# Flamingo block on one core: Wv and Wout loaded in halves, row statistics on GpSimd, a step's scales in one chain

## The reference

```python
x = x + tanh(g_xattn) * ((context @ Wv) @ Wout + bout)     # attention with that mask
h = layernorm(layernorm(x)) * ln1_g + ln1_b                # 256 wide
h = gelu(fake_quant(h) @ fake_quant_weight(w1).T + b1)     # 1024 wide
h = layernorm(h) * ln2_g + ln2_b
x = x + tanh(g_ffn) * (fake_quant(h) @ fake_quant_weight(w2).T + b2)
```

## Time and profile before

| | us |
|---|---|
| median of three runs | 402.39 |
| the profiled execution, its own time | 400.17 |
| its span, first to last instruction | 398.4 |
| VectorE busy | 330.2 (83%) |
| TensorE busy | 304.1 (76%) |
| ScalarE busy | 277.9 (70%) |
| GpSimd busy | 220.9 (55%) |
| mean granted TensorE clock | 0.949 of 2.4 GHz |

### The profile page before, as it was taken

The page is one execution under the profiler, slowest core; times in us unless marked ns, Lnnn a source line. Parts: engine busy times, 40 slices in busy tenths (PEclk is TensorE's granted clock), DMA queues, the critical chain, the costliest instruction groups (busy, mean ns, idle before and its releaser), DMA issues. The chain is left out here.

```text
span 398.4 us, 5821 instructions
## 1 busy us (share of the span) xinstructions
PE 304.1 (76%) x1690; PEld 187.9 (47%) x1690; DVE 330.2 (83%) x794; ACT 277.9 (70%) x446; POOL 220.9 (55%) x118
## 2 busy tenths in 40 slices
PE   2887295868888888888888888888888766758364
PEld 2776153434646464646464646464646342414043
DVE  0389366888999999999999999999999995957782
ACT  1314447678697979797979797979797968678431
POOL 4021444829484848484848484848485858454600
PEclk9999689989999999999999999999999996969669
DMA  7665404119183828383838383838270707062635
GB/s 226 244 225 181 132 0 130 56 53 185 54 186 107 190 102 182 108 183 110 184 107 184 108 183 109 180 111 172 67 170 18 170 17 160 26 115 71 135 77 160
DMA packets 97686, 51.56 MB, mean 129 GB/s; under 512 B 86535, under 2 KB 88768, under 8 KB 97654
## 3 DMA queue, kind: packets, MB, share of 16 engines
q1 hardware_dynamic: 96758, 51.14, 50.7%
q10 hardware_dynamic: 896, 0.04, 0.1%
HBM read 21.78 MB, written 8.41 MB: 76 GB/s over the span
## 5 line engine op out<-in xcount | busy, mean ns | idle before, releaser
L337 POOL TENSOR_TENSOR y<-u,g_bc 128x1024 f32<-128x1024 f32 x64 | 150.3, 2368 | 62.5 <-DVE parts L594 49.7
L694 DVE TENSOR_TENSOR y<-y,slot_c 128x1024 f32<-128x1024 f32 x64 | 77.7, 1214 | 9.9 <-PE slot_c L965 9.8
L698 DVE TENSOR_REDUCE amax<-y 128x1 f32<-128x1024 f32 x64 | 78.1, 1220 | 2.2
L432 ACT ACTIVATE q<-y,s 128x1024 f16<-128x1024 f32 x64 | 69.8, 1139 | 11.5 <-DVE s L725 11.5
L459 ACT ACTIVATE junk<-u,usum 128x1024 bf16<-128x1024 f32 x64 | 73.5, 1149 | 2.1
L1003 PE MATMUL bank_f<-w2T,q2T 128*128 128x256 f16 x512 | 66.1, 276 | 2.6 <-DVE res L745 2.4
L320 POOL TENSOR_TENSOR rstd<-var,half_neg 128x8 f32<-128x8 f32 x18 | 29.5, 1641 | 69.0 <-DVE var L645 56.6
L965 PE MATMUL slot_c<-ln_rows,rows 128*128 128x512 bf16 x128 | 41.3, 406 | 30.8 <-DVE y L694 16.3
L944 PE MATMUL bank_q<-wvo,ctxT 128*128 128x256 f32 x232 | 59.7, 387 | 0.0
L1003 PEld LDWEIGHTS bank_f<-w2T,q2T 128*128 128x128 f16 x512 | 50.2, 99 | 14.6 <-DVE res L745 4.8
L423 ACT ACTIVATE q<-h,s 128x256 f16<-128x256 f32 x64 | 27.3, 496 | 32.7 <-DVE s L685 32.7
(11 more groups left out here) (114 smaller groups left out, 426.8 us busy)
## 6 DMA issues: line engine op xcount, KB each, us to landing
c_in<-in_ctx SPq DMA_DIRECT2D x16, 512.0 KB, 3.4
x_in<-in_x SPq DMA_DIRECT2D x16, 512.0 KB, 4.1
out<-res SPq DMA_DIRECT2D x32, 256.0 KB, 2.8
y<-in_L_ffn_w SPq DMA_DIRECT2D x2, 1024.0 KB, 9.3
u<-in_L_xattn_Wkv SPq DMA_DIRECT2D x1, 1024.0 KB, 6.8
u<-in_L_xattn_Wout SPq DMA_DIRECT2D x1, 1024.0 KB, 10.0
q2T<-q SPq DMA_TRANSPOSE x64, 3.3
g_bc<-in_L_ffn_ln_g SPq DMA_DIRECT2D x1, 512.0 KB, 4.5
```

The lines of the kernel that those rows point to most:

```text
L337: nc.gpsimd.tensor_tensor(y[:, k % 2, t, :], u[:, t, :], g2_bc[:, :], ALU.mult).then_inc(gain2_done, 1)
L432: nc.scalar.activation(q2[:, t, :], y[:, k % 2, t, :], ACT.Copy, scale=s2[:, t:t + 1]).then_inc(q2_done, 1)
L694: nc.vector.tensor_tensor(line, line, slot_c[:, :], ALU.add).then_inc(y_done, 1)
L698: nc.vector.tensor_reduce(amax2[:, t:t + 1], y[:, k % 2, t, :], AX.X, ALU.max, apply_absolute_value=True).then_inc(amax2_done, 1)
```

## The change

The statistics' chain moves from VectorE to GpSimd: `deviations`, `split` and `variance`, and the end of the old `join` as `norm_first`. VectorE keeps four bn_aggr (`join`), and `first` and `second` become one chain `scales` of six instructions over both norms. y has three buffers instead of two, rows two instead of one. `attention` uses `slot_a` for slices from 3 on. Wv and Wout come in two halves each; w2 is prepared in body 0, its copies on VectorE. `quantise` of tiles 2 and 3 moves behind the squares, their transposes and products into the next body, and there is one more body (18) on every engine. The orders below are those of the changed kernel.

```diff
@@ set-up and SyncE
-        y = sb("y", [P, 2, T, H])
+        y = sb("y", [P, 3, T, H])
-        rows = sb("rows", [P, 2, P], BF16)
+        rows = sb("rows", [P, 2, 2, P], BF16)
-        bodies = range(-3, S + 2)
+        bodies = range(-3, S + 3)
+            for n in range(2):
+                cols = slice(512 * n, 512 * (n + 1))
+                sp.dma_start(wv_raw[:, :, cols], ...).then_inc(wv_in[n], 16)
+                sp.dma_start(wout_raw[:, 4 * n:4 * n + 4, :], ...).then_inc(wout_in[n], 16)
             for i in bodies:
+                if live(i - 3):
+                    store(i - 3, 0)
+                    turn_second(i - 3, 2)
+                    turn_second(i - 3, 3)
                 if live(i):
                     turn_first(i)
-                if live(i - 2):
-                    for t in range(T):
-                        turn_second(i - 2, t)
-                if live(i - 3):
-                    store(i - 3, 0)
-                    store(i - 3, 1)
                 if live(i + 4) and i + 4 > 1:
                     load_x(i + 4)
-                if live(i + 5) and i + 5 > 1:
+                if live(i + 5) and i + 5 > 2:
                     load_context(i + 5)
-            store(S - 1, 0)
-            store(S - 1, 1)
+                if live(i - 2):
+                    turn_second(i - 2, 0)
+                    turn_second(i - 2, 1)
+                if live(i - 3):
+                    store(i - 3, 1)
@@ GpSimd, body(i)
+                def norm_first(k):
+                    wait(pool, moments_done, k + 1)
...
+                    nc.gpsimd.tensor_scalar(stat[:, 0, :], moments[:, :, 0], -1.0, None, ALU.mult)
+                    nc.gpsimd.tensor_scalar(var[:, 0, :], moments[:, :, 1], 1.0 + LN_EPS,
+                                            LN_EPS * LN_EPS, ALU.mult, ALU.add) \
+                        .then_inc(var1_done, 1)
+                def variance(k):
+                    wait(pool, square_done, T * k + T)
...
+                def split(n):
+                    if n == 0:
+                        wait(pool, std_done, min(i + 2, S + 2))
...
+                        wait(pool, scales_ready, scales_after(i - 1))
...
                 if -1 <= i <= S:
-                    wait(pool, split_steps, split_count(i))
+                    deviations()
+                if -1 <= i <= S + 1:
+                    for n in range(5):
+                        split(n)
...
                 if live(i - 1):
-                    if i > 1:
-                        gain(i - 1, 2)
                     gain(i - 1, 3)
                 if live(i + 1) and i > -1:
                     gain_first(i + 1)
+                if live(i + 2) and i > 0:
+                    norm_first(i + 2)
                 if live(i):
                     gain(i, 0)
                     gain(i, 1)
+                    gain(i, 2)
+                if live(i):
+                    variance(i)
                 if -1 <= i + 1 <= S:
                     root(i + 1)
@@ ScalarE, body(i) from 1 on
+                if 0 < i <= S:
+                    take_rows()
+                if live(i + 3) and i > 0:
+                    take_context(i + 3, 0)
                 if live(i - 2):
                     quantise(i - 2, 0)
                     quantise(i - 2, 1)
+                if live(i + 3) and i > 0:
+                    take_context(i + 3, 1)
+                if live(i):
+                    for t in range(T):
+                        gelu(t)
+                        square(t)
                 if live(i - 2):
                     quantise(i - 2, 2)
                     quantise(i - 2, 3)
@@ VectorE
+                def join(k):
...
+                    for t in range(T):
+                        op = nc.vector.bn_aggr(moments[:, t, :], bn[:, t, :])
+                    op.then_inc(moments_done, 1)
+                def scales(kinds=slice(0, 2), those=slice(0, T)):
...
+                    nc.vector.tensor_tensor(amax_g[one], amax[one], power, ALU.mult) \
+                        .then_inc(scale_steps, 1)
...
@@ VectorE, body 0
                     shift_first(1)
+                    first_max(1)
+                    scales()
+                    sum_weights(1)
                     residual(2, 0)
...
+                    join(2)
+                    scale_weights(1)
+                    round_weights(1, 0)
+                    round_weights(1, 1)
+                    weight_copy(0)
+                    weight_copy(1)
@@ VectorE, body(i) from 1 on: residual and statistics of i+2, then
                 if live(i - 1):
                     row(i - 1, 0)
+                    if live(i + 2):
+                        join(i + 2)
                     row_max(i - 1, 0)
                     row(i - 1, 1)
                     row_max(i - 1, 1)
                     if i == S:
+                        scales(slice(1, 2), slice(0, 2))
                     row(i - 1, 2)
                     row_max(i - 1, 2)
+                if live(i - 3):
+                    final(i - 3, 2)
+                    final(i - 3, 3)
                 if live(i - 1):
                     row(i - 1, 3)
                     row_max(i - 1, 3)
+                if i == S:
+                    scales(slice(1, 2), slice(2, 4))
+                if live(i + 1):
+                    shift_first(i + 1)
+                    first_max(i + 1)
                 if live(i - 2):
                     final(i - 2, 0)
                     final(i - 2, 1)
                 if live(i + 1):
+                    scales()
@@ TensorE, body 0 and body(i) from 1 on
+                    for t in range(T):
+                        hidden(t)
+                    pe.wait_ge(x1_done, 6)
+                    sum_weights(1)
                     turn_context(3, 0)
+                    turn_weights(1, 0)
                     turn_context(3, 1)
+                    turn_weights(1, 1)
                     attention(3, 0)
+                    attention(3, 1)
                     return
...
+                if live(i + 3):
+                    turn_context(i + 3, 0)
                 if i <= S + 1:
                     turn_rows()
                 if live(i - 1):
                     correction(i - 1, 0)
+                if live(i + 3):
+                    turn_context(i + 3, 1)
+                if live(i - 3):
+                    second_product(i - 3, 2)
+                if live(i - 1):
+                    correction(i - 1, 1)
                 if live(i):
                     hidden(0)
                 if live(i - 1):
+                    correction(i - 1, 2)
                 if live(i):
                     hidden(1)
+                if live(i - 3):
+                    second_product(i - 3, 3)
                 if live(i - 1):
+                    correction(i - 1, 3)
                 if live(i):
                     hidden(2)
                     hidden(3)
                 if live(i + 1):
                     shift_first(i + 1)
                 if live(i - 2):
+                    second_product(i - 2, 0)
                     second_product(i - 2, 1)
                 if live(i + 3):
                     attention(i + 3, 0)
+                    attention(i + 3, 1)
```

More of the change, by code:

```diff
@@ L493, in body @@
                     take_rows()
[L494 to L503 removed]
                 if i == 0:
                     take_context(3, 0)
[L506 to L510 removed]
+                    take_context(3, 1)
             for i in bodies:
@@ L836, in body @@
                     if i == S:
-                        for n in range(4):
-                            second(i - 1, n, slice(0, 2))
+                        scales(slice(1, 2), slice(0, 2))
                     row(i - 1, 2)
                     row_max(i - 1, 2)
+                if live(i - 3):
+                    final(i - 3, 2)
+                    final(i - 3, 3)
                 if live(i - 1):
@@ L847, in body @@
                 if live(i + 1):
-                    shift_first(i + 1)
-                for n in range(4):
-                    if live(i + 2):
-                        join(i + 2, n)
-                if live(i):
-                    variance(i)
-                if live(i + 1):
-                    first(i + 1, 0)
-                for n in range(4):
-                    if i == S:
-                        second(i - 1, n, slice(2, 4))
-                    elif live(i - 1):
-                        second(i - 1, n)
-                    if live(i + 1):
-                        first(i + 1, n + 1)
+                    scales()
+                if i == S - 1:
+                    scales(slice(1, 2))
             for i in bodies:
                 body(i)
-            body(S + 2)
         @block.tensor
         def _(pe):
-            pe.wait_ge(consts, 9)
-            pe.wait_ge(wv_in, 16)
-            for n, slot in enumerate((slot_a, slot_b)):
-                for m in range(4):
-                    for k in range(KD):
-                        turned = nc.tensor.transpose(
```

(6 more changed lines are left out.)

558 lines of the change are left out of this document (232 added, 326 removed).

## The result

The changed kernel is **slower**: 414.0 us median of four runs (413.0 to 415.3) against 402.3 of the kernel before on the same chip, a ratio of 1.030 with a 95% interval of 1.026 to 1.035. The forecast was 394.1 in a range of 383 to 412. Some executions of a kernel take longer at a lower granted clock, and every ratio in this document leaves these out. The profiled execution has a span of 411.7 us (398.4 before) and a mean granted TensorE clock of 0.893 (0.949 before).

What follows compares the result with a forecast made beforehand. VectorE was taken to set the pace, busy 19.15 of 20 us per step. Start -3.0, steps -14.5, gelu(0) to last square of slice 15 -0.5, end +9.7 sum to -8.3: 402.4 to 394.1 us, range 383 to 412.

Steps and rivals of the forecast that it cites:

- The start: Up to gelu(0) of slice 1: 3 us earlier than 73.91, between 5 earlier and 1 later; taken as -3.0.
- blocked 2.3 once: Body 0, VectorE's `scales`: held up a single time by a gain on GpSimd, costing 2.3 us.
- the turning of w2: Body 0: VectorE's two copies of w2, 1.2 us each, would each wait about 1 us for TensorE's turning.
- The steps: Fourteen steps between gelu(0) of slices 1 and 15: 19.0 us each plus 3, 269.0 against 283.5, so -14.5.
- The loop from row to row: From the end of row(i-1, 1) through TensorE, ScalarE, GpSimd and VectorE to the next row 1: 19.0 us per step.
- the rest fits into this loop: All other work of a step finds room in 19.0 us, with TensorE having 16.3 us of work.
- item 2 of the loop: ScalarE in each step: gelu and square of tiles 2 and 3, 2 x 2.39, ending at 9.4 us.
- the forecast's three signs of being wrong: VectorE still busy all through a step; a split taking 0.5 us; 31 us from the last square to the end.
- The end: After the last square of slice 15: stores in SyncE's queue delay transposes, 40.0 against 30.3 us, +9.7, between +6 and +11.
- The slower rival: GpSimd's small instructions in each step are 0.2 us dearer each: loop 20.6, time 416; chance 0.25 of ending above 404.4.
- The colliding ports: In each step scales slip into gain(i, 2): 1 to 2 us per step, about 409 to 420; chance 0.05.

Runs made afterwards that it cites:

- the filled kernel: The changed kernel with seven unread products in TensorE's gap ahead of the wait for the splits, bodies 2 to 13: 405.3 us, ratio 1.0083.
- three repairs: The changed kernel with TensorE's gap filled, transposes ahead of stores at the end, and body 0's gains behind its scales, together: 392.9 us, ratio 0.9783.

## Why the prediction was wrong

**The start, -3.0 forecast, +3.3 measured.** Up to slice 0 the forecast held: its gelu(0) starts at 48.7, 3.5 us earlier than before (3 to 4 forecast). All of the miss lies behind it, in body 0 and the head of body 1. One step that failed there is "blocked 2.3 once": the sum took one block, the trace shows two (2.22 and 2.17). Moving the gains away brought about 3 us (73.4 against 76.4 as the means of four traces each). Another is the turning of w2: I allowed about 1 us each, and they took 1.97 and 1.58, in a stretch of lower clock. `quantise_first(1)` starts at 66.8 (forecast 62 to 64). The second block and the two turnings make up 3.8 of the 6.3 us. Behind the copies, VectorE's two residuals of slice 3 wait 0.78 and 0.35 for attention(3), for which the forecast has no term; how much of the rest that is was not tested. The Trainium skill, SBUF — State Buffer, section Who interferes with whom, has the sum over w2 (a reduction, one SBUF input) free of such blocks and an instruction with two SBUF inputs open to them; the trace agrees: the reduction beside the third gain took 2.27, and the scale instruction that multiplies two operands took 2.17 for 8 elements.

**The steps, 19.0 forecast.** This is the larger miss: -15.0 forecast for slices 1 to 15, -2.8 measured. The loop from row to row was right as a mechanism and nearly in size: 19.2 where the clock is full, with GpSimd's five splits at 1.68 (1.65), four bn_aggr at 0.37 (0.4), VectorE down by 31 us (30). The step that failed is that the rest fits into this loop: it took all of TensorE's durations from the earlier trace rows, at the full clock. The forecast itself put TensorE behind the splits, but never asked what a wait of 1.6 us does to it. In a slow step another path ends last. It does not enter ScalarE at tile 2, as item 2 of the loop has it, but at tile 0: TensorE's second product, correction and hidden(0) behind the rows run at the lower clock, gelu(0) starts 8.3 us behind `deviations` instead of 6.7, and four tiles follow without a wait. The clock then cost 1.2 us in most steps: slices 1 to 15 took 291.4 instead of 281.1 in the filled kernel. None of the forecast's three signs of being wrong came up; none of them looks at the clock. The kernel before was idle in the same place for 1.17 and 0.79 us with four groups of products between, and its granted clock in the earlier trace rows is 1.00:

```profile
149.02 0.28 PE L941 MATMUL bank_q<-bout_rows,ones_b 128*128 128x256 bf16 x1 [1.17 <-DVE x L608]
...
152.04 0.61 PE L965 MATMUL slot_c<-ln_rows,rows 128*128 128x512 bf16 x2 [0.79 <-ACT rows L442]
```

**The end, +9.7 forecast, +12.8 measured.** The mechanism was right: transposes issued right behind each store (four behind store(14, 0), since two of slice 15 were ready, and two behind store(15, 0)), TensorE waiting for q2T (2.75 and 4.83 us), and the queue's order, undone, gave 10.0 back. `scales` ended 19.2 us behind the last square, just as forecast. The 3 us beyond it are again products at the lower clock: the two tiles behind the first wait took 3.35 us and the two behind the second 3.79, where 2.1 each was used. How near this term came is in part luck: in five traces with this order of the queue the end took 42.3 to 45.8 us, and what makes that difference was not looked into.

**The rivals.** The slower rival had the right sign for the wrong reason: its dearer small instructions did not come (0.19 to 0.30 us each in the steps). The colliding ports came in body 0 only; no scale instruction of the steps takes over 0.3 us. Of the excess of 21.6 us over the forecast span, 6.3 lie in the start, 12.2 in slices 1 to 15 and 3.1 in the end; three repairs, each for one of the causes, took away 18.7 us of span in their longest execution and 21.1 of the median.

**What stays open.** Three of the ten steps of the changed kernel between 110.3 and 310.2 kept their full clock, and the length of the gap doesn't say which: the first gap here led into a step of 20.4 us, the second into one of 19.2.

```profile
151.47 0.28 PE L918 MATMUL slot_c<-ident_b,parts 128*128 128x128 bf16 x2 [1.32 <-POOL parts L385]
...
232.99 0.28 PE L918 MATMUL slot_c<-ident_b,parts 128*128 128x128 bf16 x2 [1.63 <-POOL parts L385]
```

What decides it there is not settled. The filled bodies and those of the kernel with three splits, which change the gap itself, kept a clock of 0.97 or more from about 107 us on.

## What to carry to other kernels

When a change moves a short chain to another engine, look at what it leaves idle: a hole in TensorE of some 1.6 us in each step was paid twice, once as a wait and once as slow products behind it, and a few products that nobody reads cost less than they gave back (10 us over the slices). A queue that issues in order must hold what others wait for ahead of what itself waits; stores ahead of transposes cost 10 us at the end of the kernel. Of a step that one trace shows 1 us longer, look first whether the same list has the same length in another kernel's trace: the start and the end of this one moved by 1 to 3 us with nothing changed in them. When the loop of a step is drawn up, write beside each link at which clock its duration was read.

## What the runs showed of the hardware

- The granted clock fell behind most gaps of 1.3 to 1.7 us, one in each step (0.92 over such a step); with gaps of 0.64 us, or filled ones, it was 0.97 to 1.00 in all steps in the middle of the kernel.
- The price of a small GpSimd instruction hardly depends on its size or kind: 0.19 to 0.30 us for 4 to 72 elements in the steps, 0.06 to 0.09 between dependent ones. The power of 8 elements is the exception, 1.67.
- Four bn_aggr took 0.37 us beside a GpSimd multiplication of 2.35 in a steady step (194.79, the other from 194.44), and the same 0.37 elsewhere (75.09): no block touched them.
- The block goes both ways. In body 0 of the changed kernel two GpSimd instructions of 4 elements took 1.17 us each, where the two of the same kind ahead of them took 0.23 and 0.19; VectorE was rounding and clipping w2 (1.28 and 1.23) at that time:

```profile
60.76 0.19 POOL L352 TENSOR_SCALAR var<-moments 128x4 f32<-128x4 f32 x1
61.03 1.17 POOL L361 TENSOR_SCALAR stat<-usum 128x4 f32<-128x4 f32 x1
62.26 1.17 POOL L362 TENSOR_SCALAR var<-usq 128x4 f32<-128x4 f32 x1
```
